# Latent attention loop: key transposes in column halves, and the context's PSUM copy on ScalarE

## The reference

```python
q_r = jnp.einsum('bshq,hqr->bhsr', q_big, W_qr)
k_r = jnp.einsum('bld,hdr->bhlr', kv_rope, W_kr)
scores = jnp.einsum('bhsr,bhlr->bhsl', q_r, k_r)
attn = jax.nn.softmax(scores, axis=-1)
ctx_c = jnp.einsum('bhsl,bld->bhsd', attn, kv_rope)
ctx_lat = jnp.einsum('bhsd,hkd->bshk', ctx_c, w_kc_kv)
out = ctx_lat.reshape(b, s, H * K) @ Wo.T
```

## Time and profile before

| | |
|---|---|
| median of three runs | 1877.05 us |
| the profiled execution, device time | 1874.54 us |
| its span | 1872.8 us |
| TensorE busy | 1471.1 us, 79% |
| VectorE busy | 1392.8 us, 74% |
| ScalarE busy | 1051.4 us, 56% |
| GpSimd busy | 644.8 us, 34% |
| latent loop, first to last denominator product | 391.14 to 984.93 us |

### The profile page before, as it was taken

The page is one execution under the profiler, slowest core; times in us unless marked ns, Lnnn a source line. Parts: engine busy times, 40 slices in busy tenths (PEclk is TensorE's granted clock), DMA queues, the critical chain, the costliest instruction groups (busy, mean ns, idle before and its releaser), DMA issues. The chain is left out here.

```text
span 1872.8 us, 39610 instructions
## 1 busy us (share of the span) xinstructions
PE 1471.1 (79%) x13436; PEld 936.1 (50%) x13436; DVE 1392.8 (74%) x2416; ACT 1051.4 (56%) x1789; POOL 644.8 (34%) x654
## 2 busy tenths in 40 slices
PE   1777876999999999999997556862687769956892
PEld 0455553444444444444446445861465547745782
DVE  6889864799998888888976772336799646667674
ACT  1777763776676767677662442431567435536461
POOL 1222212164554545454500254551333110027242
PEclk9766556999999999999998678985899779958896
DMA  6920000112112121212100153433000010023334
GB/s 157 334 101 1 1 1 33 36 34 62 54 51 64 46 69 46 69 46 62 54 26 2 40 150 124 142 116 103 1 1 0 1 26 1 0 87 130 103 109 157
DMA packets 93387, 123.63 MB, mean 66 GB/s; under 512 B 22945, under 2 KB 74217, under 8 KB 92867
## 3 DMA queue, kind: packets, MB, share of 16 engines
q1 hardware_dynamic: 83395, 98.88, 18.7%
q0 software_dynamic: 7776, 21.28, 3.2%
q10 hardware_dynamic: 2112, 2.10, 0.3%
HBM read 66.85 MB, written 40.30 MB: 57 GB/s over the span
## 5 line engine op out<-in xcount | busy, mean ns | idle before, releaser
L2638 DVE TENSOR_TENSOR lat_dsum<-lat_dsum,lat_Pb 125x896 f32<-125x896 f32 x320 | 477.7, 1493 | 39.3 <-ACT lat_Pb L2577 31.1
L2577 ACT ACTIVATE lat_Pb<-banks 125x896 f32<-125x896 f32 x384 | 329.3, 928 | 188.7 <-PE banks L2474 157.7
L2452 PE MATMUL banks<-lat_Pb,lat_kv 125*64 125x448 f32 x1536 | 311.4, 548 | 5.9 <-ACT lat_Pb L2577 3.0
L2474 PE MATMUL banks<-lat_QH,lat_kT 64*125 64x448 f16 x1536 | 246.9, 362 | 5.1 <-DVE lat_QT L2602 2.1
L2452 PEld LDWEIGHTS banks<-lat_Pb,lat_kv 125*64 125x64 f32 x1536 | 104.6, 137 | 157.0 <-issue 133.2
L2474 PEld LDWEIGHTS banks<-lat_QH,lat_kT 64*125 64x125 f16 x1536 | 104.2, 132 | 138.8 <-issue 66.2
L2409 POOL TENSOR_TENSOR lat_kk<-lat_rot,lat_kk 125x768 f16<-125x768 f32 x32 | 63.9, 1996 | 291.5 <-ACT lat_kk L2544 291.5
L2975 POOL DMA_INDIRECT sent_outputs<-moe_yb,moe_yidx x98 | 98.4, 1004 | 130.1 <-ACT moe_yb L3232 107.0
L2474 PE MATMUL banks<-lat_QL,lat_kT 64*125 64x448 f16 x768 | 135.4, 349 | 0.0
L3113 PE MATMUL banks<-moe_w2d,moe_gT 88*128 (+3 forms) x780 | 103.5, 284 | 21.5 <-DVE moe_gT L3450 13.2
L3438 DVE COPY moe_xTb<-banks 128x1024 f16<-128x1024 f16 x49 | 33.7, 688 | 89.3 <-PE banks L3080 54.0
(11 more groups left out here) (446 smaller groups left out, 3267.3 us busy)
## 6 DMA issues: line engine op xcount, KB each, us to landing
moe_xb<-sent_rows SPq DMA_DIRECT2D x49, 257.0 KB
lat_raw<-in_ctx_dram SPq DMA_DIRECT2D x32, 375.0 KB
sent_rows<-zero SPq DMA_DIRECT2D x1, 7453.0 KB, 49.0
lat_QH<-lat_QT SPq DMA_DIRECT2D x64, 112.0 KB, 2.8
lat_QL<-lat_QT SPq DMA_DIRECT2D x64, 112.0 KB, 4.9
lat_rD<-lat_reciprocals SPq DMA_DIRECT2D x62, 112.0 KB, 2.8
moe_arena<-sent_outputs SPq DMA_DIRECT2D x12, 512.0 KB, 6.5
sent_rows<-zero SPq DMA_DIRECT2D x1, 5140.0 KB, 64.5
```

What stands on the lines that cost most here:

```text
L2452: ins = nc.tensor.matmul(ps[u * DC:(u + 1) * DC, 6, 0:8 * T], kv[:, par, tt, :], Pb[:, tile_slot(tt, par), u, :], start=tt == 0, stop=tt = ...
L2474: ins = nc.tensor.matmul(ps[0:KP, n % 3 * 2 + q, 0:8 * T], kT[rows, par, 2 * pair + low, 0:KP], Q[rows, par, 8 * u:8 * u + 8, :].rearrange ...
L2577: nc.scalar.activation(Pb[:, slot:slot + 2, u, :], ps[0:KP, n % 3 * 2:n % 3 * 2 + 2, 0:8 * T], ACT.Exp, scale=1.0 / QSCALE).then_inc(exp_d ...
L2638: ins = nc.vector.tensor_tensor(dsum[:, par], dsum[:, par], Pb[:, tile_slot(tt, par)], ALU.add)
```

## The change

Four edits, all in the latent loop. `turn` makes each transpose as two: the first 64 columns of `kk` go to partitions 0 to 63 of bank 7, the others to partitions 64 to 127, so that the weights are 125x64 and lie in one column half of the array each. Ahead of the transposes TensorE increments a new semaphore, for which nothing waits. `keep_context` moves from VectorE to ScalarE as an activation Copy with the same two waits. Its place on VectorE was after the sum of tile 2; on ScalarE it is ahead of the wait for score 4.

```diff
-            pv_kept = sem("context_kept")
+            pv_kept, turn_begun = sem("context_kept"), sem("key_turns_begun")
@@ turn
                             pe.wait_ge(den_kept, b - 1)
+                        pe.sem_inc(turn_begun, 1)
                         bank = ps[:, 7, :].bitcast(F16)
                         for tt in range(8 * c, min(8 * c + 8, KT)):
                             n = tt - 8 * c
-                            ins = nc.tensor.transpose(
-                                bank[:, n * KS:n * KS + KP],
-                                kk[:, par, tt], id16[0:KP, 0:KP])
+                            for q in range(2):
+                                rows = slice(q * DC, (q + 1) * DC)
+                                ins = nc.tensor.transpose(
+                                    bank[rows, n * KS:n * KS + KP],
+                                    kk[:, par, tt, rows], id16[0:KP, 0:KP])
                         ins.then_inc(kT_done, 1)
@@ ScalarE
+                    def keep_context(b):
+                        act.wait_ge(pv_done, (b + 1) * KT)
+                        if past(b, 1):
+                            act.wait_ge(ct_made, b)
+                        nc.scalar.activation(pv[:], ps[:, 6, 0:8 * T], ACT.Copy).then_inc(pv_kept, 1)
+
@@ ScalarE, body
                             slot = tile_slot(2 * pair, par)
+                            if n == 4 and past(b, 1):
+                                keep_context(b - 1)
                             act.wait_ge(s_done, b * KT + (n + 1))
@@ VectorE
-                    def keep_context(b):
-                        dve.wait_ge(pv_done, (b + 1) * KT)
-                        if past(b, 1):
-                            dve.wait_ge(ct_made, b)
-                        nc.vector.tensor_copy(pv[:], ps[:, 6, 0:8 * T]).then_inc(pv_kept, 1)
-
@@ VectorE, body
-                            if tt == 2 and past(b, 1):
-                                keep_context(b - 1)
```

## The result

The changed kernel takes 1870.55 us in the median of 11 runs (1865.2 to 1882.07); the kernel before, on the same chip, 1878.97 (1873.39 to 1887.03, 11 runs). The ratio is 0.995, 95% interval 0.9933 to 0.9968: 0.5% faster, 8.4 us by the medians, where 14.2 us were forecast. Timed again on another chip (in the table of the experiments) the ratio was 0.9924, 0.99 to 0.9949, which is 12.4 us by the medians. The profiled execution took 1873.22 us, with a span of 1871.5.

A forecast was written before the change was run, and what follows sets the result against it. TensorE was taken to set the pace in regular units, VectorE in the slower early ones. 6.7 us from the turns plus 7.5 from the copy made 14.2 off 1877.05, forecasting 1862.8 us; range 1857 to 1873.

The forecast's parts named there:

- the turns: TensorE's key-tile transposes between scores and values: half turns remove a pause and an unhidden weight load, 6.7 us off.
- regular unit: One batch element of the latent loop where TensorE sets the pace: 19.00 us, forecast to become 18.78.
- The increment: New TensorE instruction ahead of each block of turns: costed at nothing, 3.1 us if exposed.
- rival with serial halves: In the turns, both halves load and stream one after the other: 0.110 us a pair, 1882.5 us in total, chance 0.09.
- what is late next: In the loop, the denominator product, waiting for VectorE's last sum, becomes the next late thing; 1.6 us of waits stay.
- ScalarE's exponential 4: Rival on ScalarE: the copy pushes this exponential by 0.54 us in each unit and TensorE stands; 1879.6 us, chance 0.04.
- the one sign of being wrong that came: At TensorE's denominator product (line 2462): growing waits for VectorE's sums would show the forecast wrong; no size given.
- The unit of 22.65 us: Slow unit near the loop's end, clock down to 0.92 after a 2 us wait; forecast to vanish with its dip.
- VectorE keeps the pace: Rival in the loop: GpSimd still slows VectorE's sums and denominators inherit the wait; 1868.6 us, chance 0.15.
- without the copy that is 18.8: Step for units paced by VectorE: 19.3 us without the one long wait, 18.8 once the copy leaves VectorE.
- The term of 7.5 us for the copy: Gain from moving the context's PSUM copy to ScalarE: 7.5 of 9.1 us not TensorE's own work; bounds 4.5 and 9.1.
- the forecast's own: The main case's own range for the whole kernel: 1860 to 1867.5 us, with 2 us to either side; chance 0.60.

The follow-up runs named there:

- halves in sequence: The changed kernel with the loops over halves and tiles in `turn` swapped; 1879.12 us, ratio 0.9972 to the kernel before.
- The filler: The changed kernel with a 128x512 memset, for which nothing waits, on VectorE where the copy had stood; 1873.41 us, ratio 0.9943 to the kernel before.
- second profile: The changed kernel, unaltered, timed and profiled again on another chip; 1864.26 us, ratio 0.9924 to the kernel before.

## Why the prediction was right and where it failed

**Right: the turns.** A regular unit was forecast at 18.78 us and is 18.73. The pause between full array and column halves is gone, the values' weights are in place (0.55, not 0.60), a block of eight takes 0.47 for a forecast 0.49, of four 0.25 for 0.26. A pair of half turns costs what a full turn cost: 0.055, not the 0.057 taken. So the term is 8.1 instead of 6.7 us, and the half turns alone measured 8.8 us by the medians. The increment costs nothing visible: the fastest pause from score to half turn is 0.28, as before. A version without it wasn't run. The rival with serial halves (0.110 a pair) did not come; even with the halves in sequence a block of eight took 0.71 us, 0.089 a pair.

**Right: what is late next.** The values no longer start 0.15 behind a copy, ScalarE's exponential 4 is not late, and the denominators inherit the wait, as the text had it. Their waits grew from 0.95 to 9.5 us, the one sign of being wrong that came. The unit of 22.65 us is gone, its clock dip only from there: it came behind the wait at the denominators (0.92 in the unit from 720.94). The rival "VectorE keeps the pace" was given 0.15 and a gain of 8.4 us; the medians measured 8.4, and 12.4 on the other chip. In mechanism it was the case that came. That its number was met to 0.1 us is luck: it had 6.7 for the turns and 1.7 for the long waits, where 8.1 and nothing measurable came.

**Wrong: the step "without the copy that is 18.8".** It took the copy's 0.53 us off VectorE's slow unit of 19.3. The slow units of the changed kernel are mostly 19.2 to 19.4 as before; first sum to reciprocal stayed at 12.33 or 12.45 us and did not fall to 11.8. The term of 7.5 us for the copy measured nothing (ratio 1.0008, 0.9991 to 1.0025: at best 1.7 us faster, so its lower bound of 4.5 is excluded too). The median still lies in the range given, 1857 to 1873, but outside the forecast's own, which with its 2 us to either side is 1858 to 1869.5. A copy worth nothing is covered only because the wide range takes in the rival's 1868.6. The rows to see it were in the earlier trace rows: the sum before the copy took 2.42 us, the sum behind it 2.17, both stretched by GpSimd, and the copy between them 0.61, the same as its 0.62 in an undisturbed unit. Here an operation that isn't stretched beside a contender, while its neighbours are, ran in their shadow. The filler shows it: 0.48 us put back cost nothing, and the sum behind it was shorter by 0.42. The Trainium skill states the rule (SBUF — State Buffer, Who interferes with whom): a VectorE instruction with two SBUF inputs contends with a GpSimd instruction that reads SBUF, and the traces agree, mostly 1.8 to 2.6 us for such a sum beside GpSimd and 1.08 alone. The copy has its one input in PSUM.

**Wrong too: what makes the slow unit.** The prediction called VectorE the pacer and named its waits for the reciprocals (7.9 us in nine units), but set them aside. They were a link of the ring, reciprocal to product to last sum, and either end of it could be moved by one number. The path through the rows' load and GpSimd, as long as that ring, stands in neither the prediction nor the expectations. That leaves a part unsettled. Slow and regular units are two regimes of the same code, and the slow one ends in a long wait of TensorE (distance of starts): 2.9 us from 718.0 in the changed kernel, 3.0 from 545.5 with half turns alone, 3.3 from 447.8 with the copy alone; in the second profile of the changed kernel it came back after the first two such waits. How such a wait comes about can be read from the traces. In all eight of them in the runs with half turns or with the copy on ScalarE the product waits 1.3 to 2.4 us for the reciprocals, and then it or the last sum behind it falls beside GpSimd's step of line 2409: in the changed kernel that step starts at 718.20, and the sum at 718.28 takes 2.52 us instead of 1.08. Why the regime starts or returns wasn't tried. It explains in kind, not in number, why kernels with the ring spread by 9 to 20 us between runs and those without it by 3 to 7.

## What to carry to other kernels

Before taking an operation off an engine, look at whether it is stretched by contention as its neighbours are: if not, it may be running in their shadow, and moving it brings nothing there. Where an engine looks saturated, follow one period of it through every wait, and look for a round trip that stands ahead of what others need. Here, moving its consumer behind that took 8.1 us off the kernel before (1875.49 to 1867.37) and 5.1 off the changed one, and an earlier start of the trip 3.8 (1864.26 to 1860.44, six runs each, whose ranges overlap), where lightening the engine by the copy took off none. And transposes next to matmuls that use column halves could take that form here at no cost.

## What the runs showed of the hardware beyond that

- Two column halves with 125 moving columns of fp16 advance in step: 16 half turns in 0.47 us, 0.055 a pair, the same as for a full-width turn.
- The halves are served apart from each other: a value matmul (654.07) of one half started ahead of three half turns of the other that stand before it in the program. In sequence, four and four still overlapped in full (0.24), eight and eight did not (0.71).
- 1.5 us less GpSimd work per regular unit made VectorE's unchanged instructions 2.0 us shorter (1.7 and 3.7 in the first ten units, where the kernel compared with has slow ones).
- A sum of VectorE that is stretched beside GpSimd ends 0.95 or 0.96 us behind the end of an instruction of GpSimd, in all 255 cases of three traces (before, changed, with the filler).
